# Square sums of the queries by DVE block transposes, and two score products moved into the next group

## The reference, cut to what matters

```
def rmsnorm(x, w, eps=EPS):
    var = jnp.mean(xf * xf, axis=-1, keepdims=True)
    return w * (xf * jax.lax.rsqrt(var + eps)).astype(x.dtype)
q = rmsnorm(q, q_norm_w);  k = rmsnorm(repeat(k, 4), k_norm_w)
scores = einsum('bhqd,bhkd->bhqk', q, k) / sqrt(128) + mask
out = einsum('bhqk,bhkd->bhqd', softmax(scores), v)
return out.reshape(...) @ o_proj_w.T
```

## Time and profile before

| | us |
|---|---|
| median of 3 runs | 2420.13 (2418.02 to 2422.52) |
| the profiled execution | 2417.93, its span 2416.1 |
| PE busy | 2332.2, 97% of the span |
| DVE busy | 1149.3, 48% |
| Pool busy | 753.2, 31% |
| mean granted clock of PE | 0.971 of 2.4 GHz |

### The profile page before, as it was taken

The page is one execution under the profiler, slowest core; times in us unless marked ns, Lnnn a source line. Parts: engine busy times, 40 slices in busy tenths (PEclk is TensorE's granted clock), DMA queues, the critical chain, the costliest instruction groups (busy, mean ns, idle before and its releaser), DMA issues.

```text
span 2416.1 us, 34601 instructions
## 1 busy us (share of the span) xinstructions
PE 2332.2 (97%) x12594; PEld 1878.0 (78%) x12594; DVE 1149.3 (48%) x1956; ACT 779.5 (32%) x1475; POOL 753.2 (31%) x709
## 2 busy tenths in 40 slices
PE   8999999997999989998999999999899999999999
PEld 6888888875555557886788888887788888888877
DVE  3444434447677633434444444445345444544456
ACT  2222222223677731222322222322132233223321
POOL 4122122202343335444222222211443333333233
PEclk9999999998999999999999999999899999999989
DMA  3111111000000123211111111110111011101000
GB/s 142 44 40 35 39 43 43 26 28 9 18 14 16 64 70 122 104 52 54 45 45 28 36 39 44 36 32 1 58 44 36 23 35 39 39 17 35 27 32 36
DMA packets 51427, 102.09 MB, mean 42 GB/s; under 512 B 8593, under 2 KB 11153, under 8 KB 50833
## 3 DMA queue, kind: packets, MB, share of 16 engines
q1 hardware_dynamic: 51344, 100.97, 12.8%
HBM read 98.85 MB, written 2.10 MB: 42 GB/s over the span
## 4 chain that ended last, share of the span: by engine, by line
PE 86%; issue 6%; DVE 3%; POOL 3%; ACT 1%; DMA 1%; SPq 0%; POOLq 0%; DVEq 0%; ACTq 0%
PE banks L261 20%; PE banks L263 19%; PE banks L262 19%; PE banks L532 7%; PE banks L585 4%; PE banks L1171 2%; PE banks L1155 2%; PE banks L544 2%; PE banks L572 2%; PE banks L1137 1%; POOL f_wl L1582 1%; PE banks L1144 1%; PE banks L1107 1%; PE banks L1123 1%; POOL f_il L1590 1%
## 5 line engine op out<-in xcount | busy, mean ns | idle before, releaser
L261 PE MATMUL banks<-xTh,wh 128*128 128x512 f32 x1024 | 421.4, 412 | 9.0 <-DVE xTl L1858 7.4
L263 PE MATMUL banks<-xTh,wl 128*128 128x512 f32 x1024 | 405.6, 396 | 0.0
L262 PE MATMUL banks<-xTl,wh 128*128 128x512 f32 x1024 | 404.1, 395 | 0.0
L261 PE MATMUL banks<-woh,oth 128*128 128x512 f32 x768 | 317.9, 414 | 1.0 <-DVE X L848 0.7
L848 DVE TENSOR_TENSOR X<-banks,X 128x512 f32<-128x512 f32 x192 | 132.6, 691 | 381.1 <-PE banks L263 381.1
L262 PE MATMUL banks<-wol,oth 128*128 128x512 f32 x768 | 306.1, 399 | 0.0
L263 PE MATMUL banks<-woh,otl 128*128 128x512 f32 x768 | 305.0, 397 | 0.0
L929 POOL TENSOR_TENSOR sc_sb<-sc_sb,rs 128x512 f32<-128x512 f32 x96 | 100.0, 1046 | 654.0 <-DVE rs L815 654.0
L672 ACT ACTIVATE q_sb<-banks 128x512 f32<-128x512 f32 x192 | 114.5, 596 | 420.4 <-PE banks L263 420.4
L261 PEld LDWEIGHTS banks<-xTh,wh 128*128 128x128 f32 x1024 | 195.8, 191 | 49.4 <-issue 9.2
L263 PEld LDWEIGHTS banks<-xTh,wl 128*128 128x128 f32 x1024 | 194.9, 190 | 44.9
(11 more groups left out here) (209 smaller groups left out, 4041.6 us busy)
## 6 DMA issues: line engine op xcount, KB each, us to landing
raw<-in_a_in SPq DMA_DIRECT2D x144, 256.0 KB, 2.7
raw<-in_a_out SPq DMA_DIRECT2D x96, 256.0 KB, 2.6
f_q<-in_f_q SPq DMA_DIRECT2D x21, 512.0 KB, 4.2
f_s<-in_f_s SPq DMA_DIRECT2D x21, 512.0 KB, 5.2
X<-in_x SPq DMA_DIRECT2D x1, 2048.0 KB, 10.5
x_craw<-in_ctx SPq DMA_DIRECT2D x8, 256.0 KB, 2.6
x_ct<-in_ctxT_pair SPq DMA_DIRECT2D x16, 128.0 KB, 2.0
f_c<-in_ctxT SPq DMA_DIRECT2D x2, 1024.0 KB, 5.2
```

The source lines that it names most:

```text
L261: nc.tensor.matmul(out, w_hi, x_hi, start=start, stop=False)
L262: nc.tensor.matmul(out, w_hi, x_lo, start=False, stop=False)
L263: return nc.tensor.matmul(out, w_lo, x_hi, start=False, stop=stop)
```

## The change

The eight products against ones are gone. After ACT has squared two units, DVE transposes each 32x32 block of the 128x1024 tile `sq` (`nc.vector.transpose`) and sums the 32 elements that have come to lie side by side. What is left is 128x32 numbers: for each partition j of a block of 32 partitions, a sum over that block's quarter of the head dimension. One fp32 product with a constant matrix `fold` adds the four quarters and divides by 128. It gives each row all 32 numbers, and DVE picks the own four-way entry with the mask `quarter` and a short reduction.

The event `SQj` is now this DVE part alone, and a new event `SSj` is the small product and the mean. The list is rewritten: SQ and SS stand apart, scores 2 and 3 move behind U_1 and U_2 of the next group, and KT, PT2, WO3 to WO6 and PV3 shift by one place here and there. The Pool's order follows: the root of couple 3 moves to the head of the next step, the value split 1 ahead of root 1, and chunk 3 ahead of root 2. ACT waits with the next square for the transpose and no longer for the product. In the last stage the output tile `g_o` gets eight slots instead of four, and the wait for a free slot goes.

```diff
     if rms:
-        ev = events("U_0 U_1 PT0- WS0- WS1- U_2 PV0- PT1- WS2- WS3- U_3 WO0- PV1- U_4 KT0 PT2- WO1- U_5 KT1 PV2- WO2- SQ0 "
-                    "U_6 PT3- U_7 WO3- SQ1 PV3- SC0 WO4- SC1 U_8 U_9 WO5- SQ2 U_10 U_11 WO6- SQ3 SC2 WO7- SC3")
+        ev = events("U_0 SS3- U_1 SC2- PT0- WS0- WS1- U_2 SC3- PV0- PT1- WS2- WS3- U_3 WO0- PV1- U_4 KT0 WO1- U_5 SQ0 KT1 PT2- "
+                    "U_6 SS0 PV2- WO2- U_7 SQ1 PT3- WO3- PV3- SS1 WO4- SC0 WO5- SC1 U_8 U_9 SQ2 WO6- SS2 U_10 U_11 SQ3 WO7-")
...
     if not project:
...
+        if rms:
+            return events("WO6-- SS3- PT0- PV0- SC2- WO7-- WS0- WS1- SC3- PT1- WS2- WS3- PV1- WO0- WO1- PT2- PV2- WO2- "
+                          "PT3- WO3- PV3- WO4- WO5- WO6- WO7-")
...
             def square_sums(i, j):
-                st.need(pe, "q_sq", 8 * i + 2 * j + 2)
+                st.need(pe, "sq_sum", 4 * i + j + 1)
...
-                for m in range(8):
-                    last = nc.tensor.matmul(pb[3][:, m:m + 1], sq[:, m, :], onecol[:, 0:1], start=True, stop=True)
-                last.then_inc(A["ss_done"], 1)
+                nc.tensor.matmul(pb[3][:, 0:32], fold[:, 0:P], sq_part[:, j % 2, :], start=True,
+                                 stop=True).then_inc(A["ss_done"], 1)
...
                 if st.rms:
-                    st.need(act, "ss_done", 4 * i + 2 * n + g // 2)
+                    st.need(act, "sq_turn", 4 * i + 2 * n + g // 2)
...
+            def q_square_sums(i, j):
+                st.need(dve, "sq_sum", 4 * i + j)
+                st.need(dve, "q_sq", 8 * i + 2 * j + 2)
+                nc.vector.transpose(sq_turned[:, :, :].rearrange("p n d -> p (n d)"),
+                                    sq[:, :, :].rearrange("p m s -> p (m s)")).then_inc(A["sq_turn"], 1)
+                st.need(dve, "ss_done", 4 * i + j - 1)
+                st.need(dve, "sq_turn", 4 * i + j + 1)
+                nc.vector.tensor_reduce(sq_part[:, j % 2, :], sq_turned[:, :, :], AX_X, ALU.add).then_inc(A["sq_sum"], 1)
...
             def q_mean_square(i, j):
                 n, c = j // 2, j % 2
                 st.need(dve, "ss_done", 4 * i + j + 1)
+                own = quarter[:, :].rearrange("p (o b) -> p o b", o=1).to_broadcast([P, 8, 4])
+                nc.vector.scalar_tensor_tensor(sq_pick[:, :, :], pb[3][:, 0:32].rearrange("p (m b) -> p m b", m=8), EPS,
+                                               own, ALU.add, ALU.mult).then_inc(A["sq_own"], 1)
                 st.need(dve, "q_rs", 4 * (i - 1) + j + 1)
-                nc.vector.tensor_scalar(qms[:, 2 * n:2 * n + 2, 4 * c:4 * c + 4],
-                                        pb[3][:, 0:8].rearrange("p (a m) -> p a m", a=2), 1.0 / HD, EPS,
-                                        ALU.mult, ALU.add).then_inc(A["ss_out"], 1)
+                st.need(dve, "sq_own", 4 * i + j + 1)
+                nc.vector.tensor_reduce(qms[:, 2 * n:2 * n + 2, 4 * c:4 * c + 4],
+                                        sq_pick[:, :, :].rearrange("p (a m) b -> p a m b", a=2), AX_X,
+                                        ALU.add).then_inc(A["ss_out"], 1)
...
                 if st.rms:
                     if before:
-                        normalise(i - 1, 2)
+                        q_root(i - 1, 3)
                     k_root(i, 0)
                     k_root(i, 1)
                     if before:
+                        normalise(i - 1, 2)
+                    k_root(i, 2)
+                    if before:
                         normalise(i - 1, 3)
-                    k_root(i, 2)
                     k_root(i, 3)
...
                     split_v(i, 0)
                     q_root(i, 0)
+                    split_v(i, 1)
                     q_root(i, 1)
-                    split_v(i, 1)
                     normalise(i, 0)
...
                     normalise(i, 1)
+                    if more:
+                        split_chunk(i + 1, 3)
                     q_root(i, 2)
                     if more:
-                        split_chunk(i + 1, 3)
                         split_chunk(i + 1, 4)
-                    q_root(i, 3)
-                    if more:
                         split_chunk(i + 1, 5)
...
             def emit(t):
-                if t >= 4:
-                    dve.wait_ge(gs[f"out{t % 4}"], 16 * (t // 4))
-                dve_normalise(dve, "ffn1", t, xtile(t), g_o[:, t % 4, :])
+                dve_normalise(dve, "ffn1", t, xtile(t), g_o[:, t, :])
```

More of the change, by code:

```diff
@@ L76, in schedule @@
     if not project:
-        return events("WO6-- " + ("" if rms else "VT1- ") + "PT0- WO7-- WS0- WS1- PV0- PT1- WS2- WS3- PV1- PT2- WO0- WO1- "
+        if rms:
+            return events("WO6-- SS3- PT0- PV0- SC2- WO7-- WS0- WS1- SC3- PT1- WS2- WS3- PV1- WO0- WO1- PT2- PV2- WO2- "
+                          "PT3- WO3- PV3- WO4- WO5- WO6- WO7-")
+        return events("WO6-- VT1- PT0- WO7-- WS0- WS1- PV0- PT1- WS2- WS3- PV1- PT2- WO0- WO1- "
                       "PV2- WO2- PT3- WO3- PV3- WO4- WO5- WO6- WO7-")
@@ L164, in program @@
             kfac = sb("kfac", [P, 1])
+            fold = sb("fold", [P, P])
+            quarter = sb("quarter", [P, 4])
+            same_row = sb("same_row", [P, 32])
+            sq_turned = sb("sq_turned", [P, 32, 32])
+            sq_part = sb("sq_part", [P, 2, 32])
+            sq_pick = sb("sq_pick", [P, 8, 4])
         with ExitStack() as sx:
@@ L252, in program @@
             g_zl = sb("g_zl", [P, NT, P], F32R)
-            g_o = sb("g_o", [P, 4, DM])
+            g_o = sb("g_o", [P, NT, DM])
         def f32(ap):
@@ L316, in program @@
             "in0", "in1", "in2", "in3", "hi", "w", "p1", "ev", "hd", "ch", "exp", "z", "zt", "zhi", "zr", "p2", "res", "xb",
-            "out0", "out1", "out2", "out3")}
+            "out")}
         def stage_end(name):
@@ L609, in run @@
                         scores(j, n)
-                    elif kind == "SQ":
+                    elif kind == "SS":
                         square_sums(j, n)
@@ L828, in run @@
                     elif kind == "SQ":
+                        q_square_sums(j, n)
+                    elif kind == "SS":
                         q_mean_square(j, n)
@@ L870, in dve_attention @@
                 dve.wait_ge(A["kf_ready"], 1)
+                nc.vector.tensor_reduce(quarter[:, :], ident[:, :].rearrange("p (b j) -> p b j", b=4), AX_X,
+                                        ALU.add).then_inc(A["fold_set"], 1)
+                nc.vector.tensor_reduce(same_row[:, :], ident[:, :].rearrange("p (b j) -> p j b", b=4), AX_X,
+                                        ALU.add).then_inc(A["fold_set"], 1)
+                dve.wait_ge(A["fold_set"], 2)
+                nc.vector.tensor_scalar(fold[:, :].rearrange("p (b j) -> p b j", b=4),
+                                        same_row[:, :].rearrange("p (o j) -> p o j", o=1).to_broadcast([P, 4, 32]),
+                                        1.0 / HD, None, ALU.mult).then_inc(A["fold_set"], 1)
+                dve.wait_ge(A["fold_set"], 3)
             run(0, order(True, False))
@@ L995, in pool_attention @@
             step(NKV - 1, True, False)
+            if st.rms:
+                q_root(NKV - 1, 3)
             normalise(NKV - 1, 2)
@@ L1649, in sp_ffn1 @@
                 sp.wait_ge(ln_done, 8 * LN_NORMS["ffn1"] + t + 1)
-                sp.dma_start(a["out"][t * P:(t + 1) * P, :], g_o[:, t % 4, :]).then_inc(gs[f"out{t % 4}"], 16)
-            for h in range(4):
-                sp.wait_ge(gs[f"out{h}"], 16 * (NT // 4))
+                sp.dma_start(a["out"][t * P:(t + 1) * P, :], g_o[:, t, :]).then_inc(gs["out"], 16)
+            sp.wait_ge(gs["out"], 16 * NT)
         def pool_split_ffn1(pool, n):
```

2 lines of the change are left out of this document (1 added, 1 removed).

## The result

The changed kernel takes 2405.23 us (median of 4 runs, 2400.70 to 2406.12), the kernel before beside it 2420.33 us (4 runs, 2418.02 to 2422.52). The ratio is 0.9935 [0.9923, 0.9946]: 15.1 us faster, by more than the measurement's 0.2%, where 41 were forecast. In the profiled executions the span falls from 2416.1 to 2404.2 us, by 11.9.

What follows compares the result with a forecast made beforehand. PE, busy 97% of the span, bounds the kernel; loop groups -17.6, clock -13.9 and +4.8, first group -12.6, tail -1.8 sum to -41: 2417.9 becomes 2377, with 2.2 for the runs' median 2379 us, range 2350 to 2408.

Steps and rivals of the forecast that it cites:

- The first group: First key-value group: 66.5 us becomes 48.9 of steps and waits plus 5 for three clock falls, so -12.6 us.
- the tail: Last query unit's end to WO2: 31.4 us becomes 26.9, with 2.7 lost at the last group's SS2: -1.8 us.
- The transpose: On DVE, per head couple: a 128x1024 block transpose takes 1.21 us, the same as the reduction.
- C: Rival on DVE: the transpose runs at half rate, 2.4 us, costing +21 us, total 2400 us; chance 0.10.
- D: Rival on DVE: the transpose goes in four passes, 4.6 us, so the kernel is slower, 2454 us; chance 0.06.
- PE's saving: Square sums on PE: 1.46 us saved a block, four blocks a group, 5.84 us a group.
- The wait at WO0: PE waits 2.4 us a group at WO0 for DVE work delayed by the moved scores; the largest new cost.
- The other waits of the group: Loop group on PE: 0.4 us at PV3, behind DVE's queued low part done at 3.8, and 0.5 at SS2.
- The clock in the loop: Loop groups: clock losses behind square sums vanish, -13.9 us; falls of 1.7 in four of ten groups add +4.8.
- A: Rival: DVE less crowded, WO0 wait under 1 us, the clock never falls: -64, 2356 us; chance 0.22.
- B: Rival: the clock falls at every new wait, two falls of 1.7 us in all seven groups: 2405 us; chance 0.12.
- E: Rival: removed products lay beside other work, so only the clock gains: 2406 us; chance 0.02.

Runs made afterwards that it cites:

- e3: Changed kernel with DVE's transpose and reduction over half the tile (512 of 1024 columns), the 16 numbers used twice: 2382.08 us, ratio 0.9855 against the kernel before.
- e5: e2 with WO5 one unit earlier, between U_10 and couple 2's small product: 2368.19 us, ratio 0.9784 against the kernel before.
- e1: Kernel before with only the changed order (scores moved, eight products kept, no folding): 2436.56 us, ratio 1.0079 against the kernel before.
- e4: Changed kernel with unread 512-column products ahead of SS1, SS2 (first group), PV1, PV2 (last pass): 2395.04 us, ratio 0.9906 against the kernel before.
- e2: Changed kernel with scores back in their own group and SQ and SS further apart: 2369.73 us, ratio 0.9799 against the kernel before.
- e6: e5 with unread 512-column products in waits of the first group, last group and last pass: 2360.75 us, ratio 0.9751 against the kernel before.

## Why the prediction was right or wrong

The direction and most parts of a loop group were right, the size was not: 29 us of the span's forecast gain are missing. The step that failed is the reckoning of the stage's two ends. The first group was put at -12.6 and the tail at -1.8. Measured are -6.4, and +11.9 from U_0 of the last group to WO2 where -5.2 had been forecast. Three things are wrong there: the waits are longer than reckoned, the half clock was put at 5 us in the first group and at nothing in the tail, and one stretch of the old kernel was counted twice. In the loop a smaller step failed, the length of the chain behind a queued DVE operation, "done 0.6 later, at 3.8".

- **The transpose: right.** 1.244 and 1.220 us for 1.21 each. Rivals C and D fall with that row. Their price of 22 us for each microsecond agrees with e3, which however tried only a shorter chain. The Trainium skill (Vector Engine (DVE) Microarchitecture Reference, "The reshape front-end and per-opcode configuration") has the transpose sustain one element a cycle and lane; the trace agrees: the 512 elements fewer of e3 take 0.53 us less.
- **PE's saving: right.** 5.84 a group; e5's group closes with it to 0.24 us.
- **The wait at WO0: right.** 2.27 + 0.25 for 2.4, and e1 and e3 show it to be the moved scores' alone. The mask add took 1.32 us behind the Pool's 1.04, and ended 0.55 behind it as was reckoned. The Trainium skill (SBUF — State Buffer, "Who interferes with whom") says that a DVE instruction with two SBUF inputs contends with a GpSimd one that reads SBUF, and that the later one is blocked; the trace agrees, with these two rows.
- **The other waits of the group: too small.** PV3 0.83 for 0.4, PV2 0.29 for 0, SS2 0.64 for 0.5. Over the six groups PE waits 24.5 us more than before, where 19.8 were counted: 4.7 of the missing gain. From the end of U_7 (PT3 begins at 1888.54) ACT's square begins at 1888.74, the transpose at 1889.44, the low part at 1891.93, and PV3 can start at 1892.74: 4.2 and not 3.8. The low part takes its whole 0.68 where 0.6 was put, and the hand-overs from PE to ACT, from ACT to DVE and from DVE to PE come to 0.20, 0.10 and 0.13 where two of 0.05 were. PV2 depends on PT2's low part in just the same way behind couple 0's fold, which is why it waits too. e3 takes all three waits away with 1.07 us less.
- **The clock in the loop: nearly right.** -7.8 for the -8.2 of six groups. Behind WO0's wait it falls in four of seven groups (1788, 1864, 2018, 2092), 1.7 us each: 6.8 for the "+4.8".
- **The first group: half.** -6.4 for -12.6. PE waits 9.3 of its 60.1 us, where 7.7 were reckoned. "3.2 for SS2" took the fold as the first thing on DVE. It stands behind `ssum`, and that behind ACT's exponential, which ACT does behind U_9's square and copy (1755.46 and 1756.30): 5.10. And PE is busy for 50.8 us, where 41.2 of work at full clock had been put, so the "three falls of the clock, 5" came to 9.6. The fall behind SS1 takes SC0, SC1 and half of U_8 with it. e4 gets 6.1 of it back by filling.
- **The sum's own fault.** "Seven groups" counted each from U_0 to the next U_0, and "the tail" began at the last query unit's end. WO6, SQ3, SC2, WO7 and SC3 of the old last group lie behind that end, together 10.9 us, and of the new one only WO7, 2.8. The seventh group's -2.5 holds that difference as well as the tail's -4.5 does: 8.1 us too much. With it the last group up to its last query unit comes to +7.4, and +7.3 was measured (67.8 to 75.1). That the two agree so closely is in part luck: PE waits there 0.5 more than reckoned and works 0.6 less.
- **The tail: wrong.** 36.0 us for 26.9 (before: 31.4). The waits are 0.64, 1.41, 5.70 and 2.53 where 0.5, 1.4, 3.9 and 1.4 were reckoned, 3.1 more, and e1 shows that the last three come from the moved scores. The other 6.0 were not put into the sum at all: it went by full clock, with 19.7 us of work, and PE was busy for 25.7 at a granted clock of 0.79. e4 recovers only 2.1 of that, so that the half clock accounts for all 6.0 is argued and not shown.

By stretch 6.2, 5.2, 8.1, 9.1 and 0.7 are the 29.3 that are missing (the 0.1 beside 29.2 is rounding).

As to the rivals: the waits refute A, and the transpose's row C and D. The measured 2405.23 is the very price of B (2405) and close to that of E (2406), and that is luck. B had 24 us of falls behind the new waits of seven groups, of which 6.8 came; E had nothing saved on PE but the clock, and PE has 51.6 us less to do. Half clock behind waits, which is B's mechanism, did cost more than forecast, but at the two ends and not in the loop.

What the prediction didn't ask, and e1 and e2 answer in part: the two halves of the change have opposite signs. The folding with the scores at home brings 50 us, and the move costs 17 by itself. Beside the folding the changed kernel lacks 35.5 against e2. The waits at WO0 and in the last pass are the move's. Those at PV3 and SS2 come from the folding where its chain is thinly covered: e1 without the folding has neither in the loop, and e2 with the folding and more cover has neither. No run has the move together with the better cover, so the 35.5 are not divided.

## What to carry to other kernels

Price a change's parts singly, each against the kernel with and without the other, and run the better half alone. Where a steady loop is bounded by two unlike ends, write the balance between fixed instructions (here U_0, U_0, WO2), so that no stretch is counted twice. A step moved over the loop's edge makes the last pass longer, and there nothing covers its chain. And when two executions are compared at a point, compare them from the start of the stage: the stage began up to 5 us apart in these runs, ahead of anything that the edits touch.

## What the runs showed of the hardware

- DVE transposes a 128x1024 tile of four-byte elements by 32x32 blocks in 1.24 us, as long as the reduction of the same tile (1.22), and 128x512 in 0.71 (e3).
- The clock went to 0.50 behind the waits of 3.3 us and more that nothing filled, and in the changed kernel behind four of seven waits of 2.0 to 2.3 us. It also went there where PE was busy all the time, behind a block of one-column fp32 products next to P.V's: e1 shows it at 1884 and 1898, with the engine 2.00 of 2.00 us busy. Without those blocks and with no wait above 1.1 us (e2, e5) the loop ran at 1.00.
- Unread products of 512 columns in a wait pay where PE waits often: 10.2 us in e4 and 7.4 in e6 by the medians; between the points around the first group 6.1 and 6.8. The Trainium skill (TensorE: Matmul & The Clock Gate, "HAM oscillation — how this bites in real kernels") tells of waits that bring the slow clock back at each burst; the trace agrees, with 0.74 against 0.91 over the same 40 us.
- A shorter gap did it too, between two blocks of 64-column products: in e4 SC1 took 3.65 us behind a gap of 1.32, and with four unread products in the gap (e6) it took 1.97. The wait of 1.10 at WO6 in e2 brought no fall.
